# Second router and experts joined to the block of the first experts and the convolution; convolution rows summed with the old rows on TensorE; adjacency loop written out

## What is computed

```python
x = x + _L0_gnn_ref(_layernorm(x), L0_gnn_W, src, dst, edge_weight)   # relu(A (x W)), A from 41250 weighted edges
x = x + _L0_ffn_ref(_layernorm(x), ...)   # attention, 8 heads; then 64 experts, 2 per token, capacity 78
x = x + _L1_gnn_ref(_layernorm(x), edge_index, L1_gnn_W_l, L1_gnn_b_l, L1_gnn_W_r, L1_gnn_gamma, L1_gnn_beta)
x = x + _L1_ffn_ref(_layernorm(x), L1_ffn_Wr, ...)   # 8 experts, 2 per token, no capacity

def _L1_gnn_ref(x, edge_index, W_l, b_l, W_r, gamma, beta):
    agg = segment_sum(x[src], dst); deg = segment_sum(1, dst)
    h = relu(agg / max(deg, 1) @ W_l.T + b_l + x @ W_r.T)
    return (h - mean(h, 0)) * rsqrt(var(h, 0) + EPS) * gamma + beta     # over the 1250 nodes

def _L1_ffn_ref(x, Wr, W1, b1, W2, b2):
    top_vals, top_idx = top_k(x @ Wr, 2); top_w = softmax(top_vals)
    for e in range(8):
        y_e = gelu(x @ W1[e] + b1[e]) @ W2[e] + b2[e]                   # added with its gate to the rows that chose e
```

## Time and profile before

| | us |
|---|---|
| median of three runs | 1403.25 (1402.82 to 1404.64) |
| the profiled execution | 1406.14 |
| its span | 1404.4 |
| adjacency stage, first to last weighted product | 51 to 190 |
| second router with its block's barriers | 1202.7 to 1257.7 |
| blocks of the second experts | 1263 to 1372 |
| mean granted clock of PE over the span | 0.975 |

### The profile page before, as it was taken

One profiled execution on the slowest core, in us unless ns is written; L12 is line 12 of the kernel. 1 busy time (PEld: TensorE's weight loads), 2 busy tenths in 40 slices (PEclk: granted clock), 3 DMA queues, 4 the chain that ended last, 5 costly groups with the idle time before them and its releaser, 6 DMA issues. The chain is left out here.

```text
span 1404.4 us, 24117 instructions
## 1 busy us (share of the span) xinstructions
PE 1345.4 (96%) x7835; PEld 888.0 (63%) x7836; DVE 751.0 (53%) x1617; ACT 452.4 (32%) x1129; POOL 339.4 (24%) x493
## 2 busy tenths in 40 slices
PE   9999999999999999999999999999989999899994
PEld 4788854455457777777566777767445555656661
DVE  6799966562168888888674333333540011643336
ACT  2699940121045555555222111111440012211110
POOL 4588830000000000000124555554100000014540
PEclk9999999999999999999999999999999999789996
DMA  6100000040010000000424999998400000732326
GB/s 162 31 0 0 0 0 0 0 183 0 0 42 2 2 1 2 1 2 1 156 78 140 332 324 321 324 315 287 161 1 0 0 0 0 251 106 92 99 82 231
DMA packets 84234, 131.00 MB, mean 93 GB/s; under 512 B 11905, under 2 KB 49175, under 8 KB 83773
## 3 DMA queue, kind: packets, MB, share of 16 engines
q1 hardware_dynamic: 70343, 108.72, 23.7%
q0 software_dynamic: 12032, 18.17, 4.1%
q10 hardware_dynamic: 1788, 3.16, 0.8%
HBM read 115.33 MB, written 29.56 MB: 103 GB/s over the span
## 5 line engine op out<-in xcount | busy, mean ns | idle before, releaser
L1265 PEld LDWEIGHTS ps<-b_r 128*128 128x128 f32 x1024 | 124.2, 192 | 33.7 <-issue 32.2
L1238 POOL TENSOR_TENSOR b_x<-b_x,b_r 125x512 f32<-125x512 f32 x10 | 12.7, 1268 | 524.9 <-DVE b_r L1495 524.9
L1265 PE MATMUL ps<-b_r 128*128 128x78 f32 x1024 | 122.2, 272 | 1.2 <-DVE b_r L1477 1.2
L1274 PE MATMUL ps<-b_r 128*78 128x512 f32 x256 | 120.3, 592 | 0.0
L634 PE MATMUL ps<-b_r 125*125 125x160 f32 x660 | 117.5, 314 | 2.1 <-ACT b_r L543 2.1
L543 ACT ACTIVATE b_r<-b_r 125x125 f32<-125x125 f32 x330 | 108.3, 389 | 6.8 <-DVE b_r L430 3.2
L1040 PEld LDWEIGHTS ps<-b_r 125*64 125x64 f32 x1600 | 85.3, 136 | 24.6 <-issue 22.8
L1433 ACT ACTIVATE b_r<-ps,b_r 128x78 f32<-128x78 f32 x128 | 34.7, 323 | 203.0 <-PE ps L1265 199.9
L1003 PE MATMUL ps<-b_r 64*125 64x417 f32 (+1 forms) x480 | 95.5, 529 | 1.4 <-DVE ps L1132 1.2
L1040 PE MATMUL ps<-b_r 125*64 125x125 f32 x1600 | 94.7, 272 | 1.3 <-ACT b_r L1068 1.3
L634 PEld LDWEIGHTS ps<-b_r 125*125 125x125 f32 x660 | 92.0, 187 | 5.5 <-ACT b_r L543 3.7
(11 more groups left out here) (287 smaller groups left out, 2344.9 us busy)
## 6 DMA issues: line engine op xcount, KB each, us to landing
b_r<-L_ffn_w SPq DMA_DIRECT2D x128, 512.0 KB, 8.4
b_r<-y SPq DMA_DIRECT2D x20, 512.0 KB, 7.7
b_r<-L_ffn_W SPq DMA_DIRECT2D x2, 4096.0 KB, 20.4
y<-b_r SPq DMA_DIRECT2D x2, 2500.0 KB
b_x<-x SPq DMA_DIRECT2D x5, 480.0 KB
rows<-b_r SPq DMA_DIRECT2D x1, 2400.0 KB
out<-b_x ACTq DMA_DIRECT2D x5, 480.0 KB
rows<-b_r SPq DMA_DIRECT2D x2, 960.0 KB
```

The source lines that it names most:

```text
L1265: last = pe.matmul(T.ps[:, 2 + r % 2, f * CAP:(f + 1) * CAP], T.ew1[r % WS][:, k, f * 128:(f + 1) * 128], T.ex_t[:, r % 2, k, :], start=(k ...
L1274: last = pe.matmul(T.ps[:CAP, 4 + r % 2, :], T.eh[:, r % 2, f, :], T.ew2[r % WS][:, f, :], start=(f == 0), stop=(f == FK - 1))
```

## The change

**Adjacency.** `visits` no longer loops over tens: the eleven bodies of ten groups stand one after another in the program, for all four engines; only the outer loop, over further windows, remains. POOL reads the column of each group in place; `next_columns`, its copy and the two waits go.

**One block.** `second_router` and `second_experts` are gone as blocks; their instructions follow in `routed_layers`, a function that also holds the first experts and the convolution. The engines do not meet any more until the end. SP loads the experts' weights when the sums of the convolution are done, and stores the normalized rows group by group.

**Rows.** The last feature part is normalized in two pieces. For each tile PE puts the old row and the four parts into one bank, as f32 matmuls with the identity; ACT copies the sum to `T.x`. Three banks are used in turn. For the first three tiles all but the last part is issued ahead. Turns and logits of group 0 stand after tiles 6 and 8.

**Router.** Logits are read from PSUM, the first eight tiles are chosen while the logits of the last two are made (`choose_of`, as in the first router), the counts are `count_in_parts`. Starts of the experts come from one masked sum (`T2.lower`), the slot of a choice from one formula, its block by rounding. POOL multiplies the tile numbers. Block numbers, choice ids and gate rows are worked out after the token ids. The fillers are 8, 3, 2, 4, 34 and 12 in number, where there were 14, 36, 13, 48 and 26.

```diff
-            peeled = 0
-            if after and peel:
-                body(0, engine.snap(seen, min_val=0, max_val=NG * WINDOWS), True)
-                engine.reg_add(seen, seen, UNROLL)
-                peeled = 1
-            with engine.Fori(0, NG // UNROLL - peeled) as q:
-                body(q * UNROLL + peeled * UNROLL, engine.snap(seen, min_val=peeled * UNROLL, max_val=NG * WINDOWS), False)
+            for g0 in range(0, NG, UNROLL):
+                body(g0, engine.snap(seen, min_val=g0, max_val=NG * WINDOWS), g0 == 0)
                 engine.reg_add(seen, seen, UNROLL)
...
-            def next_columns(g0, seen):
-                pool.wait_ge(S.pool_sources, seen)
-                pool.tensor_copy(T.ten_columns, T.lo_col[:, bass.ds(g0, UNROLL), VJ]).then_inc(S.columns_taken, UNROLL)
...
-                    pool.wait_ge(S.columns_taken, seen + UNROLL)
...
-                    pool.tensor_scalar(T.sources[:, i % 2, VJ], T.lo_iota[:], T.ten_columns[:, i:i + 1], None, ALU.is_equal)\
+                    pool.tensor_scalar(T.sources[:, i % 2, VJ], T.lo_iota[:], T.lo_col[:, g0 + i, VJ:VJ + 1], None, ALU.is_equal)\
...
+            sp.wait_ge(S.sums_done, KD * 3)
+            sp.dma_start(T.w1, A.L1_ffn_W1.rearrange("e (k p) f -> p e k f", k=KD)).then_inc(S.w12_loaded, 16)
...
+            def rows_before(t):
+                pe.matmul(T.ps[:P, t % 3, :], T.ident[:P, :P], T.x[:, t, :], start=True, stop=False)
+
+            def conv_rows_of(t, parts):
+                for m in parts:
+                    last = pe.matmul(T.ps[:P, t % 3, m * 128:(m + 1) * 128], T.conv[:, m, t * P:(t + 1) * P], T.ident[:],
+                                     start=False, stop=(m == KD - 1))
+                return last
+
             pe.wait_ge(S.conv_relu, KD * 3)
-            keep_busy(pe, T, 7, 14)
+            pe.wait_ge(S.conv_normed, KD - 1)
+            for t in range(3):
+                rows_before(t)
+                conv_rows_of(t, range(KD - 1))
+            keep_busy(pe, T, 7, 8)
             pe.wait_ge(S.conv_normed, KD)
...
+            pe.wait_ge(S.wr_loaded, 32)
+            for t in range(NT):
+                if t == 4:
+                    pe.wait_ge(S.conv_normed, KD + 1)
+                if t >= 3:
+                    pe.wait_ge(S.conv_added, t - 2)
+                    rows_before(t)
+                conv_rows_of(t, range(KD) if t >= 3 else (KD - 1,)).then_inc(S.conv_turned, 1)
+                if t == 6:
+                    transpose_group(pe, T, T.rows_b, S.f_rows, S, 3, 0, 3, 3)
+                if t == 8:
+                    logits_in(0)
+            keep_busy(pe, T, 7, 3)
+            transpose_group(pe, T, T.rows_b, S.f_rows, S, 3, 1, 3, 3)
+            logits_in(1)
+            keep_busy(pe, T, 1, 2)
+            transpose_group(pe, T, T.rows_b, S.f_rows, S, 3, 2, 3, 3)
+            keep_busy(pe, T, 1, 4)
+            logits_in(2)
...
+            count_in_parts(pe, T2, E1, SPLIT, 2, S.chosen, S.counted)
+            keep_busy(pe, T, 0, 34)
+            pe.wait_ge(S.partitions_placed, 2 * TOP)
+            pe.wait_ge(S.placed, 2 * (1 + TOP))
+            make_table(pe, T2, 7, BR, NB).then_inc(S.table_made, 1)
+            make_choices(pe, T2, 3, BR, T2.place, NB).then_inc(S.table_made, 1)
+            keep_busy(pe, T, 0, 12)
+            pe.wait_ge(S.w12_loaded, 32)
+            block_turn(0, 0)
+            pe.wait_ge(S.gates_ready, 2)
...
+            for t in range(NT):
+                act.wait_ge(S.conv_turned, t + 1)
+                act.activation(T.x[:, t, :], T.ps[:P, t % 3, :], ACT.Copy).then_inc(S.conv_added, 1)
+                row_roots(act, T, S, 3, [t])
+                if t == 6:
+                    copy_group(act, T, T.feats, S, 3, 0, 3, 3)
+            copy_group(act, T, T.feats, S, 3, 1, 3, 3)
...
+            for t in range(NT):
+                dve.wait_ge(S.conv_added, t + 1)
+                row_moments(dve, link, T, T.x, t, S.rows_var)
+                if t > 0:
+                    router_input(t - 1)
+            router_input(NT - 1)
...
+            link(dve.tensor_tensor(T2.fewer, T2.lower, totals.unsqueeze(1).to_broadcast([P, E1, E1]), ALU.mult))
+            link(dve.tensor_reduce(first, T2.fewer, AX.X, ALU.add))
...
+            place_in_rows(dve, T2, BR, row, S.placed)
+
+            dve.wait_ge(S.gap_exp, 2)
+            gates(dve, link, T)
+            dve.wait_ge(S.table_made, 1 + TOP)
+            token_ids(dve, link, T2, 7, BR, NB).then_inc(S.ids_ready, 1)
```

More of the change, by code:

```diff
@@ L247, in graph_convolution, with visits @@
     PAIRS = NT // 2
-    def visits(engine, name, body, before=None, after=None, peel=True):
+    def visits(engine, name, body, before=None, after=None):
         count = engine.alloc_register(name + "_passes")
@@ L704, in gates, with count_in_parts @@
     link(dve.tensor_tensor(T.gate[:, :, 1], T.gate[:, :, 0], T.gap[:], ALU.mult))
[L707 to L722 removed]
+def count_in_parts(pe, T, experts, split, begun, chosen, done):
     def counts(t0, t1):
@@ L1180, in logits_of, with loops_of, blocks, is_first @@
         return T.ps[:P, LOGITS[g], (t - 4 * g) * E0:(t - 4 * g + 1) * E0]
+    FK1 = F1 // 128
+    SLOTS1 = 4
+    def loops_of(engine):
+        return engine.value_load(T.loops[0:1, 0:1], min_val=FOURS - 2, max_val=NB // 4 - 2)
+    def blocks(engine, step):
+        loops = loops_of(engine)
+        for r in range(4):
+            step(0, r)
+        with engine.Fori(0, loops) as q:
+            for r in range(4, 8):
+                step(q, r)
+        for r in range(4, 8):
+            step(loops, r, last=(r == 7))
+        return loops, 7
+    def is_first(q, r):
+        return isinstance(q, int) and 4 * q + r == 0
+    def expert_of(engine, q, r):
+        return engine.value_load(T.block_expert[0:1, bass.ds(q * 4 + r, 1)], min_val=0, max_val=E1 - 1)
+    def second_logits(t):
+        g = t // 4
+        return T.ps[:P, (6, 7, 0)[g], (t - 4 * g) * E1:(t - 4 * g + 1) * E1]
     with nc.Block() as block:
@@ new lines, in block_hidden @@
+            def block_hidden(q, r):
+                e = expert_of(pe, q, r)
+                wait_count(pe, S.rx_copied, q, 4, r + 1)
+                wait_count(pe, S.rh_summed, q, 4, r - 1)
+                for k in range(KD):
+                    last = pe.matmul(T.ps[:, 2 + r % 2, 0:F1], T.rx_t[:, r % 2, k, :],
+                                     T.w1[:, bass.ds(e, 1), k, :].rearrange("p o f -> p (o f)"),
+                                     start=(k == 0), stop=(k == KD - 1))
+                last.then_inc(S.rh_done, 1)
@@ new lines, in block_step, with logits_in @@
+            def block_step(q, r, last=False):
+                if not is_first(q, r):
+                    turn_hidden(q, r - 1)
+                block_hidden(q, r)
+                if not last:
+                    block_turn(q, r + 1)
+                if not is_first(q, r):
+                    block_output(q, r - 1)
+            def logits_in(g):
+                pe.wait_ge(S.tiles_copied, turns_before(3) + (g + 1) * KD)
+                for t in tiles_of(g):
+                    for k in range(KD):
+                        last = pe.matmul(second_logits(t), T.feats[:, k, t * P:(t + 1) * P], T.w_r1[:, k, :],
+                                         start=(k == 0), stop=(k == KD - 1))
+                last.then_inc(S.logits_done, 1)
@@ new lines, in _ @@
+            link(dve.tensor_reduce(totals, T2.below, AX.X, ALU.add))
+            link(dve.tensor_tensor(T2.fewer, T2.lower, totals.unsqueeze(1).to_broadcast([P, E1, E1]), ALU.mult))
+            link(dve.tensor_reduce(first, T2.fewer, AX.X, ALU.add))
+            for b in range(2):
+                last = dve.scalar_tensor_tensor(out=T2.slots[:, 5 * b:5 * b + 5, :], in0=first.unsqueeze(1).to_broadcast([P, 5, E1]),
+                                                scalar=float(BR), in1=T.ps[:P, 2 + b, 0:5 * E1].rearrange("p (t e) -> p t e", t=5),
+                                                op0=ALU.mult, op1=ALU.add)
@@ new lines, in _ @@
+            link(last)
+            for j in range(TOP):
+                last = dve.tensor_tensor(T2.slot_of[:, j], T2.onehot[:, j, :, 0:E1], T2.slots, ALU.mult)
+            link(last)
+            for j in range(TOP):
+                last = dve.tensor_reduce(T.position[:, :, j], T2.slot_of[:, j], AX.X, ALU.add)
+            link(last)
+            within, row = T.keep, T.scratch
+            link(dve.tensor_scalar(within[:], T.position[:], (BR - 1) / 2, 1.0 / BR, ALU.subtract, ALU.mult))
+            link(dve.tensor_scalar(within[:], within[:], TO_WHOLE, None, ALU.add))
@@ new lines, in _ @@
+            link(dve.tensor_scalar(within[:], within[:], TO_WHOLE, None, ALU.subtract))
+            for j in range(TOP):
+                last = dve.tensor_tensor(T2.place[:, j], T.block_iota[:P].unsqueeze(1).to_broadcast([P, NT, NB]),
+                                         within[:, :, j].unsqueeze(2).to_broadcast([P, NT, NB]), ALU.is_equal)
```

(4 more changed lines are left out.)

545 lines of the change are left out of this document (205 added, 340 removed).

## The result

| | us |
|---|---|
| before, median of nine runs | 1404.27 (1402.13 to 1411.75) |
| after, median of nine runs | 1398.19 (1390.96 to 1402.08) |
| ratio | 0.995, interval 0.9927 to 0.9972 |
| forecast | 1388, range 1378 to 1398 |
| the profiled execution of after, its span | 1392.21, 1390.3 |

Faster, as forecast, but by 6 us instead of 15.5. The profiled execution is one of the quicker ones, so I compare stages with several profiles, and sums with medians.

A forecast was written before the change was run, and what follows sets the result against it. TensorE is busy 96% of the span, partly with fillers; four lock-step engines bound the adjacency, one engine at a time the second stretch. 8.5 + 7 = 15.5 us off the 1403.25 median gave 1388, range 1378 to 1398.

The forecast's parts named there:

- Adjacency: Loop of ten-group passes written out: ten loop edges save 8.5 us, ends nothing and 12; no gain has chance 0.11.
- Late code: Rival, chance 0.10: written-out adjacency needs 11 code packets; at 2.1 us each, 23 us lost and result 1411.
- Second stretch: Last convolution matmul to first block of second experts: 7 us less, about 11 with clock held, other end 3.
- First row: Row stage: advance work on three tiles delays the first row by some 3 us, to 1198.7.
- Tile step: Row stage: ACT's copy, DVE's moments and ACT's root add up in one chain, 1.97 us a tile with hops.
- Last normalization: End of row stage: last row normalized at 1225.1, 5.7 us later than before.
- the bank and the logits ahead of tile 9: Row stage: fourth bank needs ACT's first copy, delaying tile 7; group 0 logits of 3.6 us precede tile 9.
- Choice and counts: Second router: choice complete at 1238.9, before 1240.66, or 1235 with the clock held; count costs the same 1.87 us.
- half clock in the row stage: Rival, chance 0.07: clock drops while rows are summed, a tile costs 3.5 us, result 1402, no change.
- Prefix and placing: After the counts: 16 DVE instructions in 3.8 us, placed after 6.6 instead of 11.5; 34 fillers start the table.
- Table to first turn: Without the second barrier: 5.9 us instead of 9.4, including 0.6 of issue.
- Gate transposes: Ten transposes of gates now stand between first turn and first hidden product: 1.1 us more.

The follow-up runs named there:

- experiment 3: After with group 0 turned after tile 7 instead of 6 and its logits behind tile 9, replacing three fillers: 1394.25 us, 0.9933 of before.
- experiment 2: After measured twice more, the second set's intended POOL register moves absent from its trace: 1395.08 and 1396.01 us, 0.9953 and 0.9949 of before.
- experiment 8: After with the early stored-rows wait and an extra unread gather, issued ahead of the wait for `blocks_placed`: 1392.51 us, one run.
- experiment 4: After with 36 fillers instead of 12 between the table and the first turn: 1393.73 us.
- experiment 9: After with group 0 turned after tile 7, its logits behind tile 9, 26 and 20 fillers, early stored-rows wait, extra gather behind column work: 1389.0 us, 0.9904 of before.
- experiment 6: After with group 0 turned after tile 7, its logits behind tile 9, DVE's work behind the first gather, 28 and 22 fillers: 1393.38 us.
- experiment 7: Three single runs on after: tile columns back on DVE, 1395.35 us; stored rows awaited early, 1392.83; that wait plus an extra unread gather, 1397.66.

## Why the prediction was off, step by step

*Adjacency: right.* Forecast 8.5. By the marks 10.3, of which 0.8 from an earlier start of the stage, so 9.5; by time, alone, 7.0 by the ratio with an interval of some 2.4 on either side, 6.1 by the medians. (12.65 less ten times 1.15 makes the upper end 11.5, where the prediction says 12.) The pace came out as 1.17, where I had taken 1.18. *Late code* did not come: between 44 and 180 us queue 8 brought 9 packets and another instruction queue 20, and the only trace of them is one idle of 0.57 us on POOL at 54.74.

*Second stretch: wrong.* Forecast 7 less; alone it is 1.7 more, with zero inside the measurement. By its terms, the mean over the profiles with the order of after, against my sum:

- *First row* 7.3 after the ReLU, measured 7.4 to 7.5. Tile step 1.97, measured 1.85. Last normalization 33.7, measured 35.7 (35.2 to 37.9): the bank and the logits ahead of tile 9 were seen, and sized at least 2 us too small.
- *Choice and counts* 49.4, measured 51.1 over ten profiles (48.9 to 53.5): as late as before the change (51.2), so the new row and logit stage as a whole gained nothing. This is the first term that failed, by 1.7 us. I had priced the f32 matmuls of the row stage at the upper clock and let the clock fall only in the last logits; in all thirteen profiles of the new row stage it falls first 20.6 to 22.2 us after the ReLU, and the tile at 1201.90 shows the price. In all thirteen, in either order, TensorE waits for the fourth bank from 18.8 to 21.1 us after the ReLU, and the clock falls between 0.5 us before the end of that wait and 1.2 us behind it. Waits in every tile, which the rival has, are not there: behind one of 0.25 at 1188.05 the profile shows TensorE without a pause until 1195.6 in after, and until 1202.27 with the order of experiment 3. So the record points at the wait of 2.25 us, but no run took it away. How often the clock falls after that goes with 48.9 or 53.5 (experiment 2); with 11 to 12 us at the lower level the counts come at 49.6 on average, 0.2 from the sum. The rival *half clock in the row stage* had the clock right in kind, at a tenth of its size. The Trainium skill, "TensorE: Matmul & The Clock Gate", section "A second HAM failure mode: psum-queue depth-cycling", describes a kernel that cycles through banks, and short, frequent idles between its groups of matmuls as what makes its clock oscillate. The trace agrees in that the clock dips for 3.4 us at 1200.6, 1210.8, 1221.1 and 1227.9 and does not stay down; frequent idles it does not show here.
- *Prefix and placing:* 16 instructions in 3.8 us, as forecast, and placed 7.6 instead of 6.6 us behind the counts. `place_in_rows` took 3.30 instead of 2.81 and POOL's part 3.85 where I had put 1.1, with both at work at once (last section). Hidden by 34 fillers of 8.78 (forecast 9.0). Table start 0.4 us later than the sum on average.
- *Table to first turn:* forecast 5.9, measured 9.0: 3.1 us, and the largest single miss. I had taken 0.6 us of issue before the gather from the earlier trace rows, where a block boundary stood ahead of it; in the one block it is 3.40. In experiment 8 the extra gather takes 2.8 of the 3.1 on itself; the step is then 6.3, 0.4 above the forecast.
- *Gate transposes:* forecast +1.1 on the blocks, measured +1.2 to +2.4. The size was near, the cause was not: with TensorE kept busy before the first turn (experiment 4) they cost nothing, and 1.3 to 2.4 us go with the lower clock around the first turn, which I had put at nothing.

Misses of 1.7 + 0.4 + 3.1 + 0.7 = 5.9 us eat the 6.7 that I had summed; by the marks 0.8 is left, by time nothing. The failed steps, then, are a row stage priced at the upper clock, the issue of the first gather at 0.6 us for 3.40, and blocks without a loss of clock. Experiment 9 takes away the second and third; the first stays (0.84 from ReLU to first turn, where after had 0.89), and the other order makes up for it. With that, 13.6 of the 15.5 us are there: 1402.58 to 1389.0.

The range has a slip of its own. Its upper end, 1398, allows 5 us for the second stretch and none for the adjacency, where the text gives 3 as the other end of the stretch; with 3 it would have been 1400. (At the other end it takes 12 for the stretch, where the text has 11.)

*What stays open.* Why the first gather of the second layer waits 3.40 us in the one long block and 0.61 behind a block boundary; only some things that it is not, and that an earlier gather takes it over, are shown, the latter in three kernels. What brings the clock down first in the row stage. Whether the gap alone is worth anything in time: the two kernels that remove only it have single runs, 1397.66 and 1392.51. How much of the 6.5 us of experiment 9 is due to each of its four edits was not taken apart.

## To carry to other kernels

When two blocks are joined, do not carry a price from behind the old boundary into the new block without a row for it: the gather was issued after 0.61 us there and after 3.40 here. Look at every gap with no releaser in the first profile after, however small, and at what it does to the engine behind it: here 2.8 us on POOL were half of an idle of 5.5 us on TensorE, and one to two more were lost in the blocks. And read one stage in several profiles before its length is used in a sum: 66.4 and 72.1 us were both this code.

## What the runs showed of the hardware

- In the one long block POOL issued its first gather of the second layer, some 260 us after its last indirect transfer, 3.40 us after its copy (3.39 to 3.40 in ten profiles); a gather of no use 3 to 14 us ahead of it took that over (3.40 to 0.58 in three), and right behind POOL's own arithmetic it showed no gap itself. It is no rule for every long pause: behind a block boundary, 262 us after the last one, it was 0.61.
- Spans of one program follow the mean granted clock: the nine runs of after went from 1389.0 us at 0.980 to 1400.2 at 0.972, 1.4 us for each 0.001. A comparison of single runs of this kernel says little below 6 us.
- DVE and POOL, both on two-input operations of SBUF at once, take longer by who starts first: POOL 0.03 us ahead, DVE's comparison takes 3.30; DVE 0.02 ahead, 2.82 and POOL 3.93; alone on DVE it is 2.82. The Trainium skill, "SBUF — State Buffer", section "Who interferes with whom", says that a DVE instruction with two SBUF inputs contends with a POOL instruction that reads SBUF, and that the order of issue decides who waits; the three rows agree.
- With TensorE idle for 3.50 us (experiment 6) or 5.3 to 5.7 us (after and seven others) ahead of the first turn, the clock was at the lower level for 3.4 to 6.8 us around it; with 0.44 and 1.52 us (experiments 4 and 9) it was not. 2.75 us (experiment 8) cost no clock, and 2.77 us (the extra gather in experiment 7) cost 6.8: the length of this idle time alone does not decide.
